# Two grouped products with a residual: the first adapter's chunks requested before the ids are known, and the head and the last slot reordered

## The reference

```python
x: (128, 64, 1024) f32        # 128 samples, 64 channels, 1024 columns
itok_B_0_15: (128,) int       # drawn from 0 to 15
itok_B_3_7:  (128,) int       # jax.random.randint(..., (128,), 3, 8): from 3 to 7
x = x + einsum('bct,bcd->bdt', x, L0_cond_weights[itok_B_0_15])   # weights (16, 64, 64)
x = x + einsum('bsi,boi->bso', x, L1_cond_weight[itok_B_3_7])     # weights (8, 1024, 1024)
```

## Time and profile before

| | |
|---|---|
| median of 3 runs | 796.29 us (796.24 to 798.08) |
| the profiled execution: its own time | 796.8 us |
| its span, first to last instruction | 795.1 us |
| mean granted TensorE clock | 0.998 |
| TensorE (PE) busy | 778.8 us, 98% |
| VectorE (DVE) busy | 590.6 us, 74% |
| ScalarE (ACT) busy | 457.1 us, 57% |
| GpSimd (POOL) busy | 254.5 us, 32% |
| DMA | 90.89 MB, mean 114 GB/s |

### The profile page before, as it was taken

How to read it: one execution, slowest core, us unless ns; L and a number is a source line. 1 busy time by engine, 2 the same in 40 slices (tenths; PEclk the granted TensorE clock), 3 DMA queues, 4 the chain that set the end, 5 groups by cost and what they waited for, 6 DMA issues and landing times.

```text
span 795.1 us, 19206 instructions
## 1 busy us (share of the span) xinstructions
PE 778.8 (98%) x3448; PEld 645.2 (81%) x3449; DVE 590.6 (74%) x706; ACT 457.1 (57%) x772; POOL 254.5 (32%) x158
## 2 busy tenths in 40 slices
PE   5999999999999999999999999999999999999996
PEld 5788888888888888888888888888888888888885
DVE  7688887788887567888876788887576756756765
ACT  3465566557656555665655566556554654654554
POOL 2444533253452212435421243452122122122110
PEclk9999999999999999999999999999999999999999
DMA  8334443444442333454333444432332233233233
GB/s 264 96 108 147 144 141 107 137 130 126 148 120 65 106 100 119 122 146 145 96 102 106 123 125 136 155 101 86 106 98 77 75 106 90 68 106 99 62 104 80
DMA packets 73955, 90.89 MB, mean 114 GB/s; under 512 B 13781, under 2 KB 64470, under 8 KB 73942
## 3 DMA queue, kind: packets, MB, share of 16 engines
q1 hardware_dynamic: 63574, 57.97, 24.0%
q10 hardware_dynamic: 10368, 32.78, 14.3%
HBM read 57.15 MB, written 33.55 MB: 114 GB/s over the span
## 4 chain that ended last, share of the span: by engine, by line
PE 96%; DMA 1%; DVE 1%; issue 0%; POOL 0%; ACT 0%; ACTq 0%; SPq 0%; DVEq 0%; POOLq 0%
PE z_ps L544 15%; PE z_ps L545 15%; PE first_ps L544 15%; PE first_ps L545 15%; PE z_ps L547 15%; PE first_ps L547 13%; PE y_ps L557 7%; DMA w_nat<-in_L_cond_weight_dram 1%; DVE y L927 0%; PE y_ps L525 0%; PE first_ps L525 0%; DVE z_parts L920 0%; ACT y L669 0%; POOL w_nat L315 0%; ACTq L215 0%
## 5 line engine op out<-in xcount | busy, mean ns | idle before, releaser
L356 POOL TENSOR_TENSOR xt_lo<-x_turned,xt_hi 128x1024 fp32r<-128x1024 f32 x61 | 146.7, 2405 | 249.9 <-ACT xt_hi L653 248.4
L544 PE MATMUL z_ps<-w_hi,xt_hi 128*128 (+1 forms) x528 | 205.8, 390 | 0.0
L544 PE MATMUL first_ps<-w_hi,xt_hi 128*128 x528 | 205.5, 389 | 0.0
L545 PE MATMUL z_ps<-w_lo,xt_hi 128*128 (+1 forms) x528 | 205.4, 389 | 0.0
L545 PE MATMUL first_ps<-w_lo,xt_hi 128*128 x528 | 205.4, 389 | 0.0
L927 DVE TENSOR_TENSOR y<-y_ps,y 64x512 f32<-64x512 f32 x254 | 174.6, 689 | 33.6 <-ACT y L669 27.7
L547 PE MATMUL z_ps<-w_hi,xt_lo 128*128 (+1 forms) x512 | 199.2, 389 | 0.0
L547 PE MATMUL first_ps<-w_hi,xt_lo 128*128 x480 | 186.7, 389 | 0.0
L669 ACT ACTIVATE y<-y_ps 64x512 f32<-64x512 f32 x254 | 150.5, 594 | 11.3 <-issue 2.2
L658 ACT ACTIVATE z_parts<-z_ps 64x512 fp32r<-64x512 f32 x132 | 78.5, 595 | 132.6 <-PE y_ps L557 93.4
L658 ACT ACTIVATE z_parts<-first_ps 64x512 fp32r<-64x512 f32 x132 | 78.5, 595 | 131.4 <-PE y_ps L557 103.6
(11 more groups left out here) (135 smaller groups left out, 360.0 us busy)
## 6 DMA issues: line engine op xcount, KB each, us to landing
x_in<-in_x_dram SPq DMA_DIRECT2D x536, 64.0 KB, 2.4
out_dram<-y ACTq DMA_DIRECT2D x124, 256.0 KB, 3.6
w_nat<-in_L_cond_weight_dram SPq DMA_DIRECT2D x128, 128.0 KB
w_nat<-in_L_cond_weight_dram SPq DMA_DIRECT2D x4, 512.0 KB, 6.6
y<-in_L_cond_weight_dram SPq DMA_DIRECT2D x2, 512.0 KB, 7.1
w_turned<-in_L_cond_weights_dram SPq DMA_DIRECT2D x2, 256.0 KB, 3.8
x_in<-in_x_dram SPq DMA_DIRECT2D x2, 256.0 KB, 4.6
x_turned<-in_L_cond_weight_dram SPq DMA_DIRECT2D x1, 512.0 KB, 5.3
```

Source lines behind the costliest of these rows:

```text
L356: nc.gpsimd.tensor_tensor(xt_lo[h][:], x_turned[h][:], xt_hi[h][:].bitcast(F32), ALU.subtract).then_inc(xt_lo_made, 1)
L544: nc.tensor.matmul(to, xt_hi[h][:, t, :], whi, start=(t == 0), stop=False)
L545: mm = nc.tensor.matmul(to, xt_hi[h][:, t, :], wlo, start=False, stop=last and not pair)
```

## The change

Head: SP requests chunks 0 to 4 of adapter 0 right behind the row of ids, before any id has arrived (`AHEAD_OF_IDS`). When the smallest id is known to be above 0, SP requests chunks 0 to 4 of the adapter that it names into the same buffers, each after the earlier load of that buffer has landed; when it is 0, it signals the second half of each semaphore instead. x of slot 0 is requested behind these, then chunks 5 to 7, and the condition weights (`w0_nat`), which stood first before, stand behind chunk 7. `TURN_ORDER` has x of slot 0 behind chunk 4. PE first runs 14 transposes of the identity whose result is not used, turns four chunks ahead of the two gathering matmuls, sums four tiles of slot 0 before the turn of chunk 7, and four behind it. DVE's low parts of chunks 0 to 4 stand between the steps of the table, ahead of `table_made`; the low part of x of slot 0 stands behind it. Whether slot 0 holds two samples is read from `first_samples_i` in place of the table.

Last slot: the second half of z is summed in two quarters of 256 columns, y is summed in three parts, each by matmuls with 64-column weights that add both contributions in the same 64 rows of PSUM, so that one copy (`take_last_y`, on ACT for one sample and on DVE for the other) takes the place of `across` and the add, and each sample's row block is stored in three DMAs. The finish of the slot before is spread between these steps.

```diff
         OWN_PLACE = 6
+        AHEAD_OF_IDS = 5
         X0 = "x of slot 0"
-        TURN_ORDER = [0, 1, X0, 2, 3, 4, 5, 6, 7]
+        TURN_ORDER = [0, 1, 2, 3, 4, X0, 5, 6, 7]
         TURN_OF = {what: i for i, what in enumerate(TURN_ORDER)}
-        FOR_FIRST_HALF = 5
+        FOR_FIRST_HALF = 6
+        LAST_TURNS = 1
+        WARMING = 14
         ids_i = sb("ids_i", [P, 2], I32)
...
         TURNS = len(first_banks)
-        last_y_banks = [z_banks[0], y_ps[1]]
+        last_y_banks = [z_banks[0], y_ps[1], y_ps[0]]
+        last_z_banks = [z_banks[1][0], z_banks[1][1], z_banks[1][0]]
+        LAST_COLUMNS = [slice(0, HALF), slice(HALF, HALF + HALF // 2), slice(HALF + HALF // 2, T)]
+        LAST_IN_BANK = [slice(0, HALF), slice(0, HALF // 2), slice(0, HALF // 2)]
+        LAST_IN_HALF = [slice(0, HALF), slice(0, HALF // 2), slice(HALF // 2, HALF)]
+        LAST_PARTS = len(LAST_COLUMNS)
...
-                pool.wait_ge(first_loaded[c], 16)
+                pool.wait_ge(first_loaded[c], 32 if c < AHEAD_OF_IDS else 16)
...
-            for c in range(4, 6):
+            for c in range(4, CHUNKS_PER_GROUP):
...
+            for c in range(AHEAD_OF_IDS):
+                sp.dma_start(first_nat[c], adapter_rows[c * P:(c + 1) * P, :]).then_inc(first_loaded[c], 16)
+            sp.wait_ge(first_known, 1)
+            first_ad = sp.value_load(first_row[0:1, 0:1], min_val=0, max_val=NAD - 1)
+            def load_first(c):
+                sp.dma_start(first_nat[c], adapter_rows[bass.ds((first_ad * CHUNKS_PER_GROUP + c) * P, P), :]
+                             ).then_inc(first_loaded[c], 16)
+            with sp.If(first_ad > 0):
+                for c in range(AHEAD_OF_IDS):
+                    sp.wait_ge(first_loaded[c], 16)
+                    load_first(c)
+            with sp.Else():
+                for c in range(AHEAD_OF_IDS):
+                    sp.sem_inc(first_loaded[c], 16)
+            sp.wait_ge(samples_made, 2)
+            _, first_samples = nc.values_load_multi_w_load_instructions(
+                first_samples_i[0:1, 0:2], engines=[sp.engine], min_val=0, max_val=B - 1,
+                skip_runtime_bounds_check_because="the table is made on the chip, of clipped indices")
+            for k, sample in enumerate(first_samples):
+                sp.dma_start(x_in[0][k * C:(k + 1) * C, :], x_rows[bass.ds(sample * C, C), :]).then_inc(x0_loaded, 16)
+            for c in range(AHEAD_OF_IDS, CHUNKS_PER_GROUP):
+                if c >= OWN_PLACE:
+                    sp.wait_ge(first_turned, NH * TURN_OF[c - OWN_PLACE] + NH)
+                load_first(c)
             with nc.allow_non_contiguous_dma(reason="rows of one condition"):
                 for lo in (0, C):
                     sp.dma_start(w0_nat[lo:lo + C], cond_rows).then_inc(w0_loaded, 16)
-            sp.wait_ge(first_known, 1)
...
-                    sp.wait_ge(first_turned, NH * TURN_OF[c - OWN_PLACE] + NH)
-                sp.dma_start(first_nat[c], adapter_rows[bass.ds((first_ad * CHUNKS_PER_GROUP + c) * P, P), :]
-                             ).then_inc(first_loaded[c], 16)
-            for c in range(2):
-                load_first(c)
...
-            for c in range(2, CHUNKS_PER_GROUP):
-                load_first(c)
...
+            for _ in range(WARMING):
+                nc.tensor.transpose(first_banks[2][0][:, 0:P], ident[:], ident[:])
...
-            turn_first(0)
+            for i in range(TURNS + 1):
+                turn_first(i)
             pe.wait_ge(hot_made, 1)
             nc.tensor.matmul(firsts_ps, hot[0], vals[:], start=True, stop=True)
             nc.tensor.matmul(seconds_ps, hot[1], vals[:], start=True, stop=True).then_inc(gathered, 1)
-            for i in range(1, len(TURN_ORDER)):
+            for i in range(TURNS + 1, len(TURN_ORDER) - LAST_TURNS):
                 turn_first(i)
-            pe.wait_ge(table_made, 1)
+            pe.wait_ge(samples_made, 2)
             stores = look_first_stores(pe)
             def first_half(pair):
                 pe.wait_ge(first_lo_made, NH * FOR_FIRST_HALF)
-                sum_z(0, 0, 0, pair)
+                sum_z(0, 0, 0, pair, range(0, KT // 2))
+                for i in range(len(TURN_ORDER) - LAST_TURNS, len(TURN_ORDER)):
+                    turn_first(i)
+                sum_z(0, 0, 0, pair, range(KT // 2, KT))
             def other_half(pair):
-                pe.wait_ge(chunk_lo_made, CHUNKS_PER_GROUP)
+                pe.wait_ge(first_lo_made, NH * len(TURN_ORDER))
                 sum_z(0, 1, 0, pair)
...
+            def sum_last_z(part, pair, tiles=range(KT)):
+                for t in tiles:
+                    whi = w_hi[:, bass.ds(buf, 1), t, LAST_COLUMNS[part]].rearrange("p a o -> p (a o)")
+                    wlo = w_lo[:, bass.ds(buf, 1), t, LAST_COLUMNS[part]].rearrange("p a o -> p (a o)")
+                    last = t == KT - 1
+                    to = last_z_banks[part][:, LAST_IN_BANK[part]]
+                    nc.tensor.matmul(to, xt_hi[1][:, t, :], whi, start=(t == 0), stop=False)
+                    mm = nc.tensor.matmul(to, xt_hi[1][:, t, :], wlo, start=False, stop=last and not pair)
+                    if pair:
+                        mm = nc.tensor.matmul(to, xt_lo[1][:, t, :], whi, start=False, stop=last)
+                if last:
+                    mm.then_inc(z_summed, 1)
+            def sum_last_y(part, pair):
+                for k in range(2):
+                    pe.wait_ge(w0_placed, 2 * s + k + 1)
+                    pe.wait_ge(z_lo_made, PER_Z * s + 2 * part + k + 1)
+                    own = k if pair else 0
+                    for w in range(2):
+                        mm = nc.tensor.matmul(last_y_banks[part][own][rows_of(0), LAST_IN_BANK[part]],
+                                              w0_parts[:, k, w * C:(w + 1) * C],
+                                              z_parts[:, min(part, 1), k, LAST_IN_HALF[part]],
+                                              start=w == 0 and (pair or k == 0), stop=w == 1 and (pair or k == 1))
+                    mm.then_inc(y_summed, 1)
             def last_half(pair):
-                sum_z(1, 1, buf, pair, range(0, KT // 2))
-                sum_y(s, pair, last_y_banks, (0,))
-                sum_z(1, 1, buf, pair, range(KT // 2, KT))
+                sum_last_z(1, pair)
+                sum_last_y(0, pair)
+                sum_last_z(2, pair, range(0, KT - 1))
                 pe.wait_ge(y_made, PER_Y * (2 * pairs_past) + (PER_Y + MADE_AHEAD))
-                sum_y(s, pair, last_y_banks, (1,))
+                sum_last_y(1, pair)
+                sum_last_z(2, pair, range(KT - 1, KT))
+                sum_last_y(2, pair)
             for_both(stores, last_half)
...
+            def take_last_y(part):
+                with act.If(stores > 1):
+                    act.wait_ge(y_summed, PER_Y * s + 2 * part + 1)
+                    nc.scalar.activation(y[1][rows_of(0), LAST_COLUMNS[part]],
+                                         last_y_banks[part][0][rows_of(0), LAST_IN_BANK[part]],
+                                         ACT.Copy).then_inc(last_made[0], 1)
+                with act.Else():
+                    act.wait_ge(y_summed, PER_Y * s + 2 * part + 2)
+                    nc.scalar.activation(y[1][rows_of(0), LAST_COLUMNS[part]],
+                                         last_y_banks[part][0][rows_of(0), LAST_IN_BANK[part]],
+                                         ACT.Copy).then_inc(last_made[0], 1)
...
+            begin_half_y(0)
+            keep_last_z_hi(1)
+            begin_half_y(1)
+            take_last_y(0)
+            take_last_y(1)
+            keep_last_z_hi(2)
+            take_last_y(2)
...
+            sum_before(0, cnt)
+            keep_first_lo(0, (0,))
+            stepped()
+            sum_before(1, sums[0])
+            keep_first_lo(0, (1,))
+            stepped()
+            sum_before(2, sums[1])
+            keep_first_lo(1, (0,))
+            stepped()
+            total = sums[2]
+            step(nc.vector.tensor_tensor(looked[:, 1:3, :], total[:], cnt[:], ALU.subtract))
+            keep_first_lo(1, (1,))
+            stepped()
+            step(nc.vector.tensor_scalar(pair_count[:, 0:1], total[0:1, 0, NAD - 1:NAD], -1.0, None, ALU.add))
             link(nc.vector.tensor_tensor(picked[:], looked[:],
                                          member[:].rearrange("p (u a) -> p u a", u=1).to_broadcast([P, 3, NAD]),
                                          ALU.mult))
-            link(nc.vector.tensor_reduce(own[:], picked[:], AX_X, ALU.add))
...
+            step(nc.vector.tensor_scalar(pair_count[:, 1:2], pair_count[:, 0:1], 1, None, ALU.logical_shift_right))
+            step(nc.vector.tensor_reduce(own[:], picked[:], AX_X, ALU.add))
+            keep_first_lo(2, (0,))
+            stepped()
+            step(nc.vector.scalar_tensor_tensor(out=pos[:], in0=own[:, 1:2], scalar=2.0, in1=own[:, 0:1],
...
+            stepped()
```

(15 more changed lines are left out.)

182 lines of the change are left out of this document (95 added, 87 removed).

## The result

The changed kernel takes 804.8 us (median of 5 runs, 803.86 to 805.78) against 796.38 us of the kernel before beside it (5 runs, 796.24 to 798.08): ratio 1.0100, 95% interval 1.0089 to 1.0111, so 8.4 us slower. I had predicted 800.9 and a range up to 803.8. The sign was right, the size was not.

A forecast was written before the change was run, and what follows sets the result against it. PE bounds the kernel (busy 778.8 of 795.1 us), its head bound by bytes. Head +5.0 and end -0.4 make +4.6: 801.4 us profiled, median from 796.3 to 800.9; range 798.6 to 803.8.

The forecast's parts named there:

- the head: Everything up to slot 1's first matmul: start moves from 34.74 to 39.7, +5.0 us, bounds +2.9 to +6.3.
- The early loads: Head: reloads queue behind early chunks, 2.1 us fixed plus 1.28 each; chunk 0 lands at 11.2 instead of 9.1.
- the rival in which they slip between: Head: second request for chunk 0 served between early ones, landing at 9.1; total 798.7 us; chance 0.10.
- The table: Head, DVE: ten low parts precede it, first at 13.6; table at 24.6 instead of 15.45, bounds 23.9 to 25.9.
- Who waits for the table: Head: x of slot 1 lands at 33.9, so slot 1 starts at 39.7; the other way gives 38.3.
- The second adapter's chunk comes late: Behind the head: chunk outlasts its 3.5 us cover and slot 2 waits 2; total 803 us; chance 0.10.
- The condition weights' place: Head: behind the chunks they land near 26, are done at 32, hidden by slot 0; POOL cover 5 us.
- The transposes: Head, PE: 14 transposes take 3.4 us, any delay hidden by the wait for chunk 0; nothing won.
- the last slot: End: PE +1.9 us at 0.133 a matmul, behind PE 2.3 less (5.2 left); net -0.4, from -1.8 to +3.1.
- Weight loads at 0.188: Last slot: weight loads bind the quarters, so the end costs +2.4 us; total 803.7; chance 0.14.

The follow-up runs named there:

- run 9: Kernel before with only the five early loads of adapter 0 and their reloads added: 803.10 against 796.83 us, +6.3, ratio 1.0078.
- run 15: As run 13, with POOL's sum for the condition weights begun only after DVE's two row steps: 803.27 us, +6.4 over the kernel before, ratio 1.0077.
- run 1: The changed kernel again, only with register waits bounded from below: 806.28 against 796.85 us for the kernel before, +9.4, ratio 1.0115.
- run 2: Changed kernel with the table row's two DVE steps ahead of the low parts of chunks 5 to 7: 803.89 us, +7.0 over the kernel before, ratio 1.0088.
- run 3: Changed kernel with 18 unused transposes keeping PE busy ahead of slot 1: 804.59 us, +7.7 over the kernel before, ratio 1.0097.
- run 8: Changed kernel keeping early chunks 0 to 4 of the wrong adapter, without requesting them again: 799.76 us, +3.1 over the kernel before, ratio 1.0041.
- run 13: As run 2, with 14 transposes in PE's wait ahead of slot 0: 803.47 against 797.06 us for the kernel before, +6.4, ratio 1.0081.
- run 14: Changed kernel with the condition weights requested first, ahead of the early loads: 807.89 us, +10.8 over the kernel before, ratio 1.0139.
- run 16: Changed kernel with POOL's subtraction for the condition weights' low parts begun only after DVE's row steps: 803.33 against 796.86 us for the kernel before, +6.5.
- run 10: As run 7, with the condition weights requested first again: 797.74 us, +0.9 over the kernel before, ratio 1.0013.
- run 12: As run 10, without the 14 transposes: 798.06 us against 797.74 for run 10.
- run 4: Changed kernel without its early loads, chunks requested once the id is known: 802.35 us, +5.5 over the kernel before, ratio 1.0072.
- run 6: Changed kernel, early loads kept, table's steps in one piece, row's steps early, gathering matmuls behind the first turn: 804.96 us, +8.3 over the kernel before.
- run 7: As run 6, without the early loads: 803.06 us, +6.4 over the kernel before, ratio 1.0085.
- run 11: As run 10, with low parts between the table's steps and gathering matmuls behind the fourth turn: 801.89 us, +5.1 over the kernel before, ratio 1.0064.
- run 5: Kernel before with only the change's last slot: 797.22 against 796.68 us, ratio 1.0003 (0.9994 to 1.0012).

## Why the prediction was wrong

On the profiled execution I had forecast 801.4 us, and it took 804.8. The end fits (-0.43 for -0.4), so all 3.4 us too many are in the head, +8.43 for +5.0: slot 1 starts 1.73 later than predicted, and up to its `sum_y` PE's clock costs 1.74.

**The early loads: mechanism right, fixed time too small.** The reloads queue behind the early loads in strict order and the first four land 1.2 to 1.3 apart, so the rival in which they slip between was refuted. But the fifth early chunk landed at 11.5 and not at 9.9, when SP issued its successor: the very first requests took 3.7 us beyond their bytes, where I had taken 2.1 from chunk 0 of the kernel before. The full rate comes late (PE, PEld, DVE, ACT and POOL first, at the end the DMA share and GB/s):

```profile
4.00:5.00 1.00, 1.00 (x7) 1.00 (x6) 0.81 (x4) 0.00 (x0) 0.00 (x0) 1.00 0.80 266
5.00:6.00 1.00, 0.78 (x4) 0.38 (x2) 0.46 (x4) 0.00 (x0) 0.00 (x0) 1.00 1.02 418
```

POOL's first add came at 12.79 instead of 11.3. Alone the loads cost 6.3 us (run 9), in another order of DVE's work than here.

**The table: right by two errors.** The first low part was 1.5 late (15.08 for 13.6), and from there to `table_i` it took 9.5 us and not 11.0. Of the 1.5 less, 0.9 is that low parts follow each other at 0.60, not at the 0.69 that each is shown to last: ten took 6.0 us and not 6.9. The other 0.6 is that I had taken off too little for steps that lie under low parts. 24.55 for 24.6 is luck, not confirmation.

**Who waits for the table: the step that failed.** Its path was right in the changed kernel, where slot 1 does wait for POOL's `xt_lo`. Without the hold, in run 15, x is there at 33.1 (33.9 predicted) and `xt_lo` at 38.8 (39.7 predicted), and what then lets slot 1 start, at 39.15, is PE's own work, which I had at 38.3. The two ways are nearly level, so the wait that I had put at 1.4 us all but vanishes when nothing else is in the way. Three terms were missing.

First, the hold. The change leaves DVE's row step where POOL's operation for the condition weights now lies, and POOL's operation was costed as hidden by slot 0 without asking whom it would hold. The step took 2.38 for 0.28; runs 1, 2, 3, 8, 13 and 14 had it as well. It goes when the operations are kept apart (runs 15 and 16), and beside a POOL operation of 0.46 us the same step took 0.41 and 0.43 (runs 10 and 12). The Trainium skill (SBUF — State Buffer, SBUF: two separate sides) says that VectorE and GpSimd share one pair of ports, which an operation of VectorE with two inputs in SBUF and one of GpSimd that reads SBUF can't hold at once, and that the loser waits for the whole instruction. The traces agree: the row's step has two such inputs and ended 0.14 to 0.15 us behind POOL's in the traces of the change and of these six runs. The change also made the second step one of two inputs (a maximum for a copy), and that is the one that was held in run 2. (There and in run 13 this second step is shown to start 0.02 to 0.04 us ahead of POOL's and was held all the same; the page would give the ports to the first.)

Second, the clock. I had PE wait ahead of slot 1 and priced only the wait. 2.44 idle us there cost another 1.6 to 1.7 up to slot 1's `sum_y` (run 3), and the 1.85 ahead of slot 0 cost as much in some traces and nothing in others. How much of hold and clock reaches the end of the kernel is less than the 3.9 us that they cost up to the first `sum_y` (48.61 for run 15's 44.73): with both taken out it is 2.0 against the change (run 15, +6.4 for +8.4) and 3.0 against run 1, whose clock fell twice.

Third, the cover behind the head. "The second adapter's chunk comes late" was a rival of mine, with 0.10 and a cover of 3.5 us. It was right about the place and I had the cover wrong: in run 15 the chunk is requested at 39.48, lands at 48.35, 8.9 us later where I allowed 5.1, and then POOL's and DVE's work for slots 2 and 3 is late by 0.3 to 0.6 a time; from the first to the third `sum_y` that makes 26.04 us for 23.57. The figure stood in the trace of the kernel before, in a line that I did not read: a chunk requested at 31.10, and POOL on it 9.4 us later.

```profile
40.46 0.46 POOL L308 TENSOR_TENSOR w_nat<-w_nat,ident 128x128 f32 x1 [8.52 <-DMA w_nat<-in_L_cond_weight_dram]
```

The DMA engines aren't full meanwhile: from 40 to 48 us of the change they move 39 to 153 GB/s. The kernel fetches this chunk in four DMAs with runs of 256 numbers, and the first adapter's chunks in whole rows of 1024; whether that is why it takes 9 us was not tested. In the changed kernel nothing of it shows, because slot 1 is late anyway. It shows in runs 2, 3, 4, 6, 7, 11, 13, 15 and 16, and it is why removing the first two terms doesn't lead to my 800.9: the four kernels that do so in part or in whole (2, 13, 15, 16) lie between +6.4 and +7.0. With the early loads loaded again and this order of the table no run came under 803.2, so the forecast was too low even without hold and clock.

**The condition weights' place.** I costed it at nothing, with 5 us of cover on POOL. In the change that holds (run 14: put back, 1.4 worse). But the cover is the late table: with the table early, the same two requests block SP's queue and cost 5.5 us (runs 7 and 10). I had looked at who waits for the data and not at who is queued behind the requests.

**The transposes, the last slot.** The transposes gained nothing, as said: the first turn still takes 1.97 us (run 1), and run 12 without them is level. The last slot came out at -0.43 us for the -0.4 predicted, and that is luck again: PE's part grew by 1.2 and not by 1.9, at 0.12 a matmul for the 0.133 taken, and what stands behind it takes 5.9 and not 5.2. Run 5 can't tell the sum from zero. Weight loads at 0.188 did not bind.

**What stays open.** Why PE's clock falls after one wait of 1.8 to 2.4 us and not after another of the same length: it fell after 1.86 (runs 1 and 2), 1.84 (run 16), 2.44 (the change) and 2.39 (runs 1 and 8), not after 1.85 (the change and run 3), 1.88 (run 6) and 2.39 (run 14). That is six of ten waits; the three filled with work did not bring it down, which speaks for the filler and is not proof of it. The terms also don't add up: alone, loads 6.3, DVE's order 4.2 and the weights' place 5.5 would make 16, and together they are 8.4. That each lengthens another way to slot 1 and hides under the longest fits the traces, but no run takes the pairs apart. No run beat the kernel before.

## What to carry to other kernels

When a step is moved, ask three things of its new neighbours, not only how long it takes there: which operation of the other engine it now meets at a shared port, which requests now stand behind its own in the queue, and what the wait that it makes does to TensorE's clock. A load on a guess costs its bytes in full when the queue is already the bound (6.3 us for five of 512 KB here), so it needs a gap in the traffic and not only idle engines. And where several paths end at nearly the same point, a term measured alone can be larger than its share, and what you get back by removing it is decided by the next path: look for that one before summing. Here it was the next chunk, and its time stood in the trace of the kernel before.

## What the runs showed of the hardware

- A VectorE step of 0.28 us with two inputs in SBUF took 2.38 to 2.55 us beside a GpSimd operation of 2.4 us, and 0.41 to 0.43 beside one of 0.46; it ended 0.14 to 0.15 behind the other each time; a turn by VectorE (one input) and low parts read from PSUM beside such operations kept their length.
- SyncE's issue of two DMAs took 0.9 to 1.5 us into an empty queue and 5.30 us right behind the last chunks (run 7), and one more small one 4.62.
- The first large requests of the kernel needed 3.7 us beyond their bytes, against the 2.1 that I had read from the request at 5.66 of the kernel before; the rate was 266 GB/s from 4 to 5 us and 418 from 5 to 6.
- TensorE's granted clock fell to 0.50 to 0.62 in stretches of 2 us after waits as short as 1.84 us, for about 3 us, in six of ten waits of 1.84 to 2.44 us ahead of slots 0 and 1; with work without use in the wait it stayed at 1.00 in all three runs that had it.
- A chunk of 512 KB requested by SyncE in four DMAs took 8.9 to 9.7 us from the first request to POOL's work on it (the kernel before, the change, run 15), in the change with the DMA engines moving 39 to 153 GB/s.
